# Rotary projection: the sum of two rotation products moves from VectorE to GpSimd, and the query join moves behind the next tile's key rotation

## The reference, cut to what matters

```python
def _rope(x, cos, sin):
    x0, x1 = (xv[..., 0], xv[..., 1])
    out = jnp.stack([x0 * cos - x1 * sin, x1 * cos + x0 * sin], axis=-1)
ct_q = x @ Wd_q_w + Wd_q_b
qt_c = heads(ct_q @ Wu_q_w + Wu_q_b)
qt_r = heads(_rope(ct_q @ Wq_r_w + Wq_r_b, cos, sin))
query = qt_c + qt_r
ct_kv = x @ Wd_kv_w + Wd_kv_b
kt_c = heads(ct_kv @ Wu_k_w + Wu_k_b)
kt_r = heads(_rope(x @ Wk_r_w + Wk_r_b, cos, sin))
key = kt_c + kt_r
value = heads(ct_kv @ Wu_v_w + Wu_v_b)
```

## Time and profile before

| what | value |
|---|---|
| runs, median (lowest to highest) | 2017.29 us (2011.09 to 2022.29) |
| the profiled execution: its time, its span | 2018.74 us, 2016.9 us |
| projection, up to the first row maximum | 0 to 144 us of the span |
| VectorE / TensorE / GpSimd busy over the whole span | 81% / 92% / 35% |

### The profile page before, as it was taken

How to read it: one execution, slowest core, us unless ns; L and a number is a source line. 1 busy time by engine, 2 the same in 40 slices (tenths; PEclk the granted TensorE clock), 3 DMA queues, 4 the chain that set the end, 5 groups by cost and what they waited for, 6 DMA issues and landing times. The chain is left out here.

```text
span 2016.9 us, 25815 instructions
## 1 busy us (share of the span) xinstructions
PE 1862.0 (92%) x7414; PEld 828.5 (41%) x7414; DVE 1627.6 (81%) x2605; ACT 1087.4 (54%) x1511; POOL 697.9 (35%) x474
## 2 busy tenths in 40 slices
PE   7998999999999999998999997788889877699998
PEld 3442332332322322324666662333334333256665
DVE  6878998998988989975555667999999999945654
ACT  5553666665666666673334435676567656323321
POOL 3561000110000000110000017999999999800000
PEclk9997999998999999999999997999999999899999
DMA  4751222221221222204110013555545546300000
GB/s 135 175 136 29 50 43 44 43 48 38 49 49 38 48 44 43 43 24 153 41 42 32 11 43 113 125 142 137 136 121 142 136 121 165 93 6 16 21 21 22
DMA packets 100394, 147.14 MB, mean 73 GB/s; under 512 B 15088, under 2 KB 54400, under 8 KB 98720
## 3 DMA queue, kind: packets, MB, share of 16 engines
q1 hardware_dynamic: 100256, 145.42, 29.1%
HBM read 114.69 MB, written 30.29 MB: 72 GB/s over the span
## 5 line engine op out<-in xcount | busy, mean ns | idle before, releaser
L871 DVE TENSOR_REDUCE mx<-max_bank 128x1 f32<-128x512 f32 x976 | 628.1, 687 | 62.4 <-PE max_bank L774 61.3
L857 ACT ACTIVATE probs<-score_bank 128x1024 f32<-128x1024 f32 x512 | 496.8, 1021 | 278.4 <-PE score_bank L788 277.6
L774 PE MATMUL max_bank<-ks,qs 96*128 96x512 bf16 x976 | 339.5, 388 | 0.0
L1671 PE MATMUL ys_bank<-outs,rec_diag 128*128 128x512 f32 x512 | 260.6, 643 | 69.9 <-POOL outs L1614 45.9
L788 PE MATMUL score_bank<-qs,ks 99*128 99x512 bf16 x1024 | 312.4, 387 | 12.8 <-issue 9.8
L1606 POOL TENSOR_TENSOR ring<-u,bc 128x1024 f32<-128x1024 f32 x128 | 300.4, 2356 | 0.1
L841 PE MATMUL o_bank<-probs,vg 128*32 128x512 f32 x2048 | 274.5, 608 | 0.0
L1812 ACT ACTIVATE a_bank<-dt,decay_s 128x512 f32<-128x512 f32 x256 | 170.7, 686 | 149.7 <-DVE ring L1936 97.4
L1614 POOL TENSOR_TENSOR outs<-ring,bc 128x1024 f32<-128x1024 f32 x102 | 239.8, 2351 | 13.8 <-DVE ring L1936 13.8
L1284 PE MATMUL y_bank_f<-wpr_f,hid_f 128*128 128x256 f32 x1024 | 236.4, 379 | 0.0
L728 POOL CAST neg_parts<-neg_max 16x128 bf16<-16x128 f32 x31 | 8.7, 282 | 641.4 <-DVE neg_max L884 641.4
(11 more groups left out here) (238 smaller groups left out, 1916.8 us busy)
## 6 DMA issues: line engine op xcount, KB each, us to landing
bc<-bc_scr SPq DMA_DIRECT2D x128, 512.0 KB, 5.0
qk_parts<-parts SPq DMA_DIRECT2D x128, 96.0 KB, 1.9
qs<-qk_parts SPq DMA_DIRECT2D x128, 64.0 KB, 4.2
o_scr<-o_sb SPq DMA_DIRECT2D x32, 256.0 KB, 2.1
ks<-qk_parts SPq DMA_DIRECT2D x16, 384.0 KB, 4.7
xn_s<-xn_scr SPq DMA_DIRECT2D x8, 515.0 KB, 6.4
x<-in_x_dram SPq DMA_DIRECT2D x8, 512.0 KB, 4.1
ks<-qk_parts SPq DMA_DIRECT2D x16, 256.0 KB, 3.7
```

Source lines behind the costliest of these rows:

```text
L774: nc.tensor.matmul(max_bank[(r + a) % MB][:], qs[r][0:SROWS, half, j, qt * P:(qt + 1) * P], ks[r][0:SROWS, j, kh * TW:(kh + 1) * TW], star ...
L857: nc.scalar.activation(probs[:, s % 2, 2 * pair:2 * pair + 2], score_bank[pair][:], ACT.Exp, scale=SOFTMAX_SCALE).then_inc(probs_ready, 1)
L871: nc.vector.tensor_reduce(mx[:, a // HU, a % HU:a % HU + 1], max_bank[(r + a) % MB][:], AX_X, ALU.max)\
L1671: mm = nc.tensor.matmul(y_bank[f][:], rec_diag[:, f * NS + n], outs[:, g % OUTS, f], start=(n == 0), stop=(n == NS - 1))
```

## The change

GpSimd gets `turn_sum`: for each side it subtracts or adds two products, in place in `rot`. VectorE's `join` then has one operation a chunk: compact projection plus bias plus that sum, straight into `full`; it waits for the new semaphore `turned_sum`. The join of the queries of tile t stands behind the key rotation of tile t + 1. `rotated` counts four a side instead of six. ScalarE's, TensorE's and SP's lists are the same as before.

```diff
+            def turn_sum(t, side):
+                n, r = t * SIDES * ROTS + (1 - side) * ROTS, rot[:, 1 - side]
+                pool.wait_ge(rotated, n + 3)
+                nc.gpsimd.tensor_tensor(r[:, 0], r[:, 0], r[:, 2], ALU.subtract).then_inc(turned_sum, 1)
+                pool.wait_ge(rotated, n + 4)
+                nc.gpsimd.tensor_tensor(r[:, 3], r[:, 3], r[:, 1], ALU.add).then_inc(turned_sum, 1)
+
             for t in range(NT):
+                turn_sum(t, 1)
                 if t:
                     lower_parts(t - 1, 0)
+                turn_sum(t, 0)
                 lower_parts(t, 1)
...
             def join(t, side):
-                n = t * SIDES * ROTS + (1 - side) * ROTS
                 bias = bcol[:, 4 + 4 * side:6 + 4 * side]
-                r = rot[:, 1 - side]
-                for c in range(DC):
-
-                    dve.wait_ge(proj_ready, t * UNITS + (COMP_K if side == 1 else COMP_Q) + c + 1)
-                    dve.wait_ge(rotated, n + (1 if c == 0 else 4))
-                    nc.vector.scalar_tensor_tensor(comp_bank[c], comp_bank[c], bias[:, c:c + 1], r[:, 3 * c],
-                                                   ALU.add, ALU.add).then_inc(rotated, 1)
                 for c in range(DC):
                     u = parts_of(side) + c
-                    dve.wait_ge(rotated, n + 5 + c)
+
+                    dve.wait_ge(proj_ready, t * UNITS + (COMP_K if side == 1 else COMP_Q) + c + 1)
+                    dve.wait_ge(turned_sum, t * CHUNKS + u + 1)
                     if t:
 
                         dve.wait_ge(rest_ready, (t - 1) * CHUNKS + u + 1)
                         dve.wait_ge(high_kept, (t - 1) * CHUNKS + u + 1)
-                    nc.vector.tensor_tensor(full[:, u], comp_bank[c], r[:, 2 - c], ALU.subtract if c == 0 else ALU.add)\
-                        .then_inc(summed, 1)
+                    nc.vector.scalar_tensor_tensor(full[:, u], comp_bank[c], bias[:, c:c + 1], rot[:, 1 - side, 3 * c],
+                                                   ALU.add, ALU.add).then_inc(summed, 1)
...
             for t in range(NT):
                 rotate(t, 1)
+                if t:
+                    join(t - 1, 0)
                 if t + 2 < NT:
                     statistics(t + 2)
                 join(t, 1)
                 if t + 2 < NT:
                     norm.finish(nc, dve, t + 2)
                 rotate(t, 0)
-                join(t, 0)
...
+            join(NT - 1, 0)
```

More of the change, by code:

```diff
@@ L173, in project @@
         summed, high_kept, mid_kept = m.sem("summed"), m.sem("high_kept"), m.sem("mid_kept")
+        turned_sum = m.sem("turned_sum")
         rest_ready, low_kept, v_kept = m.sem("rest_ready"), m.sem("low_kept"), m.sem("v_kept")
@@ L193, in project @@
         UNITS = 12
-        ROTS = 6
+        ROTS = 4
         OUT = 16 * NG
```

## The result

| what | before | after |
|---|---|---|
| runs, median (lowest to highest) | 2016.97 us (2010.1 to 2064.21), 18 runs | 2026.26 us (2020.06 to 2032.86), 18 runs |
| the profiled execution: its time, its span | 2018.74 us, 2016.9 us | 2021.43 us, 2019.6 us |
| first row maximum (the projection's end) | 144.04 us | 151.30 us |

The ratio after to before is 1.0049, with a 95% interval of 1.0033 to 1.0065. It leaves out one run of the kernel before, that of 2064.21 us, which fell into a slower state of the chip. On 2016.97 us that is a loss of 9.9 us (6.7 to 13.1); the plain difference of the two medians is 9.3. The forecast was 2023 with a range of 2016.5 to 2030, most likely a small loss within 0.5%. The loss is real and inside the range, at the very edge of what I had called "within 0.5%", and nearly twice the 5.4 us that I had worked out.

A forecast was written before the change was run, and what follows sets the result against it. TensorE was taken to bound a plain tile (14.62 us), after the change a ring of 16.26; the first row maximum 5.4 us late gives 2018.74 + 5.4 = 2024.1, less 1.45 for the median: 2022.7, rounded to 2023, range 2016.5 to 2030.

The forecast's parts named there:

- TensorE bounds a plain tile, VectorE's relief is worth nothing: Projection: TensorE's 14.62 us set a plain tile, so VectorE's saved 20.4 us in all count as nothing.
- The ring of 16.26 us: Projection tile: a round through GpSimd, ScalarE and VectorE takes 11.24 + 4.88 + 0.14 us, 1.64 over TensorE's 14.62.
- blocked `finish`: VectorE's four small operations before the query rotation: the first may be held by GpSimd's low parts, 0.14 us a round.
- The price of a sum, a step of 1.12: GpSimd's new sums: 1.12 us from start to start, 1.16 for the last of a row.
- The stall carried through SP's list: Tile 5: stack loads, writes and TensorE's resumption all move by 5.46 us; the 4.9 us wait absorbs nothing.
- GpSimd without a gap from about 119: Tiles 6 and 7: GpSimd never waits, 26 operations after 119.23 us to the last query sum at 148.43.
- The first row maximum at 149.46: Projection's end: first row maximum at 149.46 us instead of 144.04, 5.4 us late.
- The x loads of tiles 5 and 6: Loads of x for tiles 5 and 6: some 3 to 5 us later, still about 2 ahead of their `statistics`.
- VectorE's relief, priced at nothing: VectorE: four operations fewer a tile at 0.68 us each, worth nothing because TensorE's work covers them.
- hidden: Rival: GpSimd's sums cost near 0.42 us a step, the round is 13.5 us, time stays 2017; chance 0.13.
- Slow sum: Rival: GpSimd's sum step counts 20 times; 0.235 us more, a step of 1.36, gives over 2028; chance 0.07.
- The clock: Rival: TensorE's idling lowers its granted clock in three of tiles 2, 3, 4, 6, giving 2028; chance 0.07.

The follow-up runs named there:

- e5: Kernel before, with SP's 26 stack loads issued in two halves, ahead of the writes of tiles 4 and 6; median 2010.09 us, ratio to before 0.9964.
- e11: Changed kernel with ScalarE's guess ahead of the queries' middle parts, guess_rs in PSUM, stack loads in two halves; median 2014.79 us, ratio to before 0.9996.
- e4: Changed kernel with each GpSimd sum over 128 of 512 columns only; one profiled execution, 2009.11 us.
- e3: Changed kernel with ScalarE's keep_xn and guess ahead of the queries' middle parts; one profiled execution, 2019.58 us.
- e10: e3 with guess_rs placed in PSUM; one profiled execution, 2021.15 us.
- e1: Kernel before with only the query join moved behind the next tile's key rotation, sums still on VectorE; one profiled execution, 2024.2 us.
- e6: Changed kernel with SP's stack loads in two halves, ahead of the writes of tiles 4 and 6; median 2022.12 us, ratio to before 1.0026.
- e9: Changed kernel with key sums written to their own tile and the query sums' second input in bfloat16; one profiled execution, 2025.93 us.

## Why the prediction was right, and where it was off

- **TensorE bounds a plain tile, VectorE's relief is worth nothing.** Right: VectorE lost 3.2 us a tile and the tile grew. e5 and e11 say it from the other side.
- **The ring of 16.26 us.** Right: measured 16.56 to 16.58. The difference is the sum's price, 4 x 0.11, less the 0.14 that I had put in for a blocked `finish`, which did not happen (all four operations last 0.16): 16.26 + 0.44 - 0.14 = 16.56. e4 and e3 with e10 show that it is this ring: with short sums, or with ScalarE's order turned and no small operation held, the tile is 14.71.
- **The price of a sum, a step of 1.12.** This is the term that was mis-sized: it is 1.23. I took it from the rests, whose second input is bfloat16, although had the all-float32 addition at 1257 ns; that row was the nearer kin. I also counted it 20 times where it counts 24: the leg from the third query product of tile 2 to the first low part of its queries holds four sums more (the query sums of tile 2, the key sums of tile 3). 24 x 0.11 is 2.6 us.
- **The stall carried through SP's list.** Right: stack loads at 81.66 (about 81), latent queries of tile 5 at 105.68 (104.99), and the wait of 5.0 us absorbed nothing.
- **GpSimd without a gap from about 119.** Right: from 120.05 to the end.
- **The first row maximum at 149.46.** Measured 151.30. By the corrected terms: 149.46 + 2.6 for the sums, less 3 x 0.14, less 0.5 since the third query product of tile 0 happened to end at 31.30 instead of 31.81 in this execution, is 151.1. The terms also fit on the way. When the stack loads begin they make 12 x 0.11 - 2 x 0.14 - 0.5 = 0.5, and 81.66 is 0.56 later than the forecast; in the last stretch they make 10 x 0.11 = 1.1, and the lateness against the forecast grows there from 0.75 to 1.84.
- **The x loads of tiles 5 and 6, late by 3 to 5 but still ahead of their `statistics`.** They are issued 4.1 and 6.0 us later (64.49 and 81.05 against 60.40 and 75.03), the second a microsecond more than I had said, and neither `statistics` waits for them. Only that of tile 7 does, in both kernels (7.09 us after, 8.28 before), under the wait of tile 5.
- **VectorE's relief, priced at nothing.** For the changed kernel the ring of the prediction is enough: e4 and e10 keep the late join and have tiles of 14.71. But the reasoning was incomplete, since I took the move for harmless by itself. e1 shows that with VectorE's sums left in place it makes the tile 15.90 and costs 6.6 us at the first maximum. So the relief is not worth nothing behind the late join: it is what removes that second ring. I had not asked what the moved join had covered, by my reading TensorE's refill of the rotary banks.
- **The median.** The forecast of 2022.7 is 3.6 below the measured 2026.26, and the forecast loss of 5.4 us lies below the whole interval of the measured one (6.7 to 13.1). The direction and the mechanism were right, the size was too small, and that 0.49% still counts as within 0.5% is luck. About 1.8 of the 3.6 is the later first maximum. The rest is not settled. The first maximum is 7.3 to 10.4 us later, depending on which executions are taken (144.04 or 141.16 before, 151.30 or 151.60 after), and the measured loss of 9.9 fits that. The profiled execution of before, on which the forecast was built, was the one with the late first maximum. For e6 the shift is 0.6 to 3.5 us against 5.2 measured (2.4 to 8.1), for e11 -7.3 to -4.5 against -0.8 (-4.4 to 2.8), for e5 -8.8 to -5.9 against -7.3 (-11.3 to -3.0). Only for e11 do the two spans not overlap, and there they just miss. With the sums on GpSimd the time may lose some us that the first maximum does not show, but this is not shown, and the single traces scatter too much behind it to say where. That stays open.

The rivals: "hidden" fell with the price of the sum (e4 shows that 0.46 us would have hidden it). "Slow sum" went the right way by 0.11, where 0.235 would have decided (0.196 with the count of 24). "The clock" did not occur: tile 3 was granted 1.00, and tile 5 had 0.85 as before. From the Trainium skill (GPSIMD Engine Reference, Engine selection), which calls GpSimd about 2x slower for two inputs, I had estimated a sum of 1.36 us; it measured 1.27 against 0.68 on VectorE, a factor of 1.9, and the page's warning was the better guide than my 1.7.

## What to carry to other kernels

Before moving work to an engine with room, follow one round through all in-order lists and count what lies between two visits of the same instruction; a count of work per engine (GpSimd's 13.9 us under TensorE's 14.6) would have let this change pass, and the tile grew to 16.6. Ask of each moved piece also what wait it used to cover. And when one wait dominates the trace (here 26 loads in one piece on a queue that writers share), take that first: a few lines there won 0.36%, where the rearrangement of three engines lost 0.49%.

## What the runs showed of the hardware

- GpSimd's two-input operation on 128x512 takes 1.27 us with two float32 inputs and 1.16 with one of them in bfloat16, in place or not (e9, and the rests); on 128x128 float32 it takes 0.456 (e4).
- A VectorE operation of 0.16 us with both inputs in SBUF can be held for a whole GpSimd operation, and a chain of them one after another: 1.07, 1.08, 1.08 (e3). It was held where it began 0.02 after the GpSimd operation (e3) and not where it began 0.01 ahead of it (e10). VectorE operations with one input in PSUM were not held: 64 rotations of 128x512 took 0.740 to 0.752 each beside a busy GpSimd (after). GpSimd was not slowed.
- Two copies of a repeated column on VectorE, 216 ns each before, took 1081 ns each where GpSimd's sums ran beside them, though a copy has only one input:

```profile
L502 DVE COPY bv_wide<-bv 128x128 f32<-128x128 f32 x2 | 2.1, 1081 | 0.0
```
